# Sum of all eight probability tiles on VectorE, ones products of 256 columns, and a rotation whose sum is made by an adding transfer from GpSimd's queue

## What is computed

```
q = (lat @ Wq)                      # lat, ctx: layer norms of x and of the context
k, v = split(ctx @ Wkv)
k = apply_rope(k, cos, sin)         # x1*cos - x2*sin, x2*cos + x1*sin, on the halves of each head
attn = softmax(clip(q @ k.T * 64**-0.5, -11, 11))
x = x + (attn @ v) @ Wo + bo
x = x + sum over 16 experts of sigmoid(x @ sel) * relu(x @ keys) @ values    # x normalized first
```

## Time and profile before

| | us |
|---|---|
| median of 3 runs (1050.04 to 1054.57) | 1051.62 |
| the profiled execution | 1056.22 |
| its span | 1054.4 |
| TensorE busy | 994.2 |
| VectorE busy | 820.1 |
| ScalarE busy | 514.7 |
| GpSimd busy | 263.4 |

### The profile page before, as it was taken

The page is one execution under the profiler, slowest core; times in us unless marked ns, Lnnn a source line. Parts: engine busy times, 40 slices in busy tenths (PEclk is TensorE's granted clock), DMA queues, the critical chain, the costliest instruction groups (busy, mean ns, idle before and its releaser), DMA issues. The chain is left out here.

```text
span 1054.4 us, 15279 instructions
## 1 busy us (share of the span) xinstructions
PE 994.2 (94%) x5336; PEld 611.8 (58%) x5336; DVE 820.1 (78%) x1235; ACT 514.7 (49%) x759; POOL 263.4 (25%) x245
## 2 busy tenths in 40 slices
PE   4599999999999999999999999999998888999998
PEld 3455555555555555555555555555553366888886
DVE  5499988999999999999889988998899754545422
ACT  5465555555556556555555555555554422222221
POOL 5443423111112121111211000321000164445443
PEclk9899999999999999999999999999999889999999
DMA  6344323332323322223322234232223163332321
GB/s 171 117 138 126 104 82 106 96 91 66 91 78 112 93 72 86 72 89 87 97 67 81 61 89 114 91 90 82 61 62 101 46 209 137 121 121 83 122 95 40
DMA packets 69369, 101.39 MB, mean 96 GB/s; under 512 B 22000, under 2 KB 44784, under 8 KB 67248
## 3 DMA queue, kind: packets, MB, share of 16 engines
q1 hardware_dynamic: 69296, 100.46, 31.4%
HBM read 70.54 MB, written 10.75 MB: 77 GB/s over the span
## 5 line engine op out<-in xcount | busy, mean ns | idle before, releaser
L1016 ACT ACTIVATE probs<-score_ps 128x1024 f32<-128x1024 f32 x256 | 249.2, 1029 | 147.9 <-PE score_ps L829 147.8
L842 PE MATMUL o_ps<-probs,v_sb 128*64 128x512 f32 x1024 | 247.7, 605 | 0.0
L1222 DVE TENSOR_SCALAR probs<-probs 128x1024 f32<-128x1024 f32 x256 | 181.4, 739 | 75.8 <-ACT probs L1016 75.8
L1231 DVE TENSOR_TENSOR p_sum<-probs 128x1024 f32<-128x1024 f32 x128 | 161.7, 1264 | 2.3
L842 PEld LDWEIGHTS o_ps<-probs,v_sb 128*64 128x64 f32 x1024 | 62.2, 136 | 112.1 <-issue 93.3
L1777 DVE SCALAR_TENSOR_TENSOR act<-h_ps,sel_all 128x512 f32<-128x512 f32 x62 | 42.8, 690 | 101.1 <-PE h_ps L142 90.3
L829 PE MATMUL score_ps<-q_hi,k_hi 64*128 64x512 f32 x512 | 115.2, 446 | 1.1 <-DVE k_lo L1201 0.8
L829 PEld LDWEIGHTS score_ps<-q_hi,k_hi 64*128 64x128 f32 x512 | 48.2, 184 | 111.4 <-issue 98.0
L1693 ACT CAST act_hi<-act 128x512 fp32r<-128x512 f32 x64 | 39.6, 620 | 143.2 <-DVE act L1777 143.2
L1545 POOL TENSOR_TENSOR act_lo<-act,act_hi 128x512 fp32r<-128x512 f32 x64 | 82.5, 1290 | 102.8 <-ACT act_hi L1693 102.8
L829 PE MATMUL score_ps<-q_hi,k_lo 64*128 64x512 f32 x512 | 101.7, 393 | 0.0
(11 more groups left out here) (197 smaller groups left out, 1950.0 us busy)
## 6 DMA issues: line engine op xcount, KB each, us to landing
sel_all<-sel_dram SPq DMA_DIRECT2D x16, 1024.0 KB, 4.8
k_swap<-k SPq DMA_DIRECT2D x124, 128.0 KB, 2.3
w_hi<-packs_hi SPq DMA_DIRECT2D x26, 384.0 KB, 4.0
w_lo<-packs_lo SPq DMA_DIRECT2D x26, 384.0 KB, 4.5
den<-inv_dram SPq DMA_DIRECT2D x64, 128.0 KB, 2.9
ctx_raw<-ctx SPq DMA_DIRECT2D x24, 128.0 KB, 2.3
packs_hi<-w_hi SPq DMA_DIRECT2D x8, 384.0 KB, 3.3
packs_lo<-w_lo SPq DMA_DIRECT2D x8, 384.0 KB, 3.6
```

The source lines that it names most:

```text
L842: mm = pe.matmul(o_ps[DH * h:DH * h + DH, :], v_sb[n // 2 % 2][:, at:at + DH], probs[s % RING][:, h, :], start=(s == 0), stop=(s == STEPS ...
L1016: act.activation(probs[s % RING][:], score_ps[s % 2][:], ACT.Exp, scale=DH ** -0.5).then_inc(exp_done, 1)
L1222: dve.tensor_scalar(probs[s % RING][:], probs[s % RING][:], CLIP_HI, CLIP_LO, ALU.min, ALU.max).then_inc(clipped, 1)
L1231: dve.tensor_tensor(p_sum[m][:], first, second, ALU.add).then_inc(summed_up, 1)
```

## The change

Three things are changed together.

- VectorE adds the two quarter sums as well (`sum_all`, 128x1024, behind the second `sum_quad`), so that `p_sum[3]` holds all eight tiles. The four ones products now take 256 columns each: block e of a head the e-th half of the queries. `den`, `den_rows`, the turning and the copy of the denominators are halved accordingly, and `invert_den` has nothing to add.
- The sum of the rotation leaves VectorE. GpSimd's queue waits for both products (`k_times`) and starts a transfer that adds k_swap to k32 (`accum_op=ALU.add`, 512 KB). The rounding of k on ScalarE and the reuse of k_swap wait for that transfer (`k_summed`).
- The wait of `sum_up` for the ones products (`den_ready`) now stands at m = 3 alone.

```diff
--- before.py
+++ after.py
@@ -97,7 +97,7 @@
 
     sh.o_raw = sb("o_raw", [P, NQ])
     sh.den = sb("den", [P, NQ])
-    sh.den_rows = sb("den_rows", [P, 2, NQ // DH])
+    sh.den_rows = sb("den_rows", [P, NQ // DH])
     sh.inv_rows = sb("inv_rows", [P, NQ // DH])
     sh.o_hi1 = sb("o_hi1", [P, NQ], F32R)
     sh.o_lo1 = sb("o_lo1", [P, NQ], F32R)
@@ -114,7 +114,6 @@
     sh.den_evac = sem("den_evac")
     sh.ident_ready = sem("ident_ready")
     sh.den_turned = sem("den_turned")
-    sh.den_added = sem("den_added")
     sh.den_inv = sem("den_inv")
     sh.inv_stored = sem("inv_stored")
     sh.inv_spread = sem("inv_spread")
@@ -159,17 +158,15 @@
     for h in range(2):
         for e in range(2):
             at = DH * h + QUAD * e
-            row = sh.den[at:at + 1, :].rearrange("a (p j) -> a p j", p=DH)
-            sp.dma_start(sh.den_rows[DH * h:DH * h + DH, e, :], row).then_inc(sh.den_turned, DMA)
+            row = sh.den[at:at + 1, 0:NQ // 2].rearrange("a (p j) -> a p j", p=QUAD)
+            sp.dma_start(sh.den_rows[at:at + QUAD, :], row).then_inc(sh.den_turned, DMA)
 
 
 def invert_den(dve, sh, n):
 
     wait(dve, sh.den_turned, 4 * DMA * (n + 1))
     wait(dve, sh.inv_stored, DMA * n)
-    dve.tensor_tensor(sh.inv_rows[:], sh.den_rows[:, 0, :], sh.den_rows[:, 1, :], ALU.add).then_inc(sh.den_added, 1)
-    wait(dve, sh.den_added, n + 1)
-    dve.reciprocal(sh.inv_rows[:], sh.inv_rows[:]).then_inc(sh.den_inv, 1)
+    dve.reciprocal(sh.inv_rows[:], sh.den_rows[:]).then_inc(sh.den_inv, 1)
 
 
 def store_inv(sp, sh, inv_dram, n):
@@ -358,6 +355,7 @@
         half_times = [sem(f"half_times{i}") for i in range(2)]
         k_times = sem("k_times")
         k_roped = sem("k_roped")
+        k_summed = sem("k_summed")
         k_hi_done = sem("k_hi_done")
         k_split = sem("k_split")
         q_projected = sem("q_projected")
@@ -370,6 +368,7 @@
         clipped = sem("clipped")
         summed_up = sem("summed_up")
         quads_up = sem("quads_up")
+        all_up = sem("all_up")
         pv_done = sem("pv_done")
         head_loaded = sem("head_loaded")
         sel_zero = sem("sel_zero")
@@ -504,7 +503,8 @@
             def swap_k(p):
 
                 sp.wait_ge(k_evac, 2 * p + 2)
-                sp.wait_ge(k_roped, p + 1)
+                sp.wait_ge(k_roped, 2)
+                wait(sp, k_summed, DMA * (p - 1))
                 for q in range(4):
                     a, b = 32 * q, 32 * (q ^ 1)
                     sp.dma_start(k_swap[a:a + 32, :], k32[b:b + 32, :]).then_inc(k_swapped, DMA)
@@ -585,7 +585,7 @@
                 if n == 29:
                     store_gates(sp, sh, sel_dram, 0)
                 if n == NPAIR - 2:
-                    sp.wait_ge(k_roped, NPAIR + 1)
+                    sp.wait_ge(k_summed, DMA * (NPAIR - 1))
                     load_keys(2)
                     load_keys(3)
 
@@ -668,6 +668,11 @@
                 pool.wait_ge(half_swapped[half], 4 * DMA)
                 part = k_half(k_swap, half)
                 pool.tensor_tensor(part, part, k_half(sin_sb, half), ALU.mult).then_inc(half_times[half], 1)
+
+            def rope_add(p):
+
+                pool.wait_ge(k_times, 2 * p)
+                pool.dma_start(k32[:], k_swap[:], accum_op=ALU.add).then_inc(k_summed, DMA)
 
             def head_norm(t):
 
@@ -708,6 +713,8 @@
                 t, p = n + FIRST_TILES, n + 1
                 if t < TILES:
                     rstd(t)
+                if p < NPAIR:
+                    rope_add(p)
                 if n + 2 < PAIRS:
                     split_weights(n + 2)
                 if n % 2 == 0 and n // 2 + 2 < DUOS:
@@ -845,15 +852,15 @@
 
             def denominators(n):
 
-                pe.wait_ge(quads_up, 2 * n + 2)
+                pe.wait_ge(all_up, n + 1)
                 pe.wait_ge(ones_ready, 1)
                 wait(pe, den_evac, n)
                 wait(pe, y_added, 2 * (n - 1))
                 for e in range(2):
                     for h in range(2):
                         at = DH * h + QUAD * e
-                        mm = pe.matmul(side_ps[at:at + QUAD, :], ones[:], p_sum[2 * e + 1][:, h, :],
-                                       start=True, stop=True)
+                        mm = pe.matmul(side_ps[at:at + QUAD, 0:NQ // 2], ones[:],
+                                       p_sum[3][:, h, e * (NQ // 2):(e + 1) * (NQ // 2)], start=True, stop=True)
                 mm.then_inc(den_ready, 1)
 
             def turn_first(t):
@@ -1002,7 +1009,7 @@
                 act.copy(v_sb[j % 2][:, at:at + 512], fill_bank(f)[:]).then_inc(v_stored, 1)
 
             def round_k(p):
-                act.wait_ge(k_roped, p + 2)
+                act.wait_ge(k_summed, DMA * p)
 
                 wait(act, scores_ready, STEPS * (p - 1))
                 act.copy(k_hi[p % 2][:], k32[:]).then_inc(k_hi_done, 1)
@@ -1024,7 +1031,7 @@
                 act.wait_ge(den_ready, n + 1)
 
                 wait(act, o_scaled, n)
-                act.copy(den[:], side_ps[:]).then_inc(den_evac, 1)
+                act.copy(den[:, 0:NQ // 2], side_ps[:, 0:NQ // 2]).then_inc(den_evac, 1)
 
             def round_weights(w):
 
@@ -1191,10 +1198,6 @@
                 dve.tensor_tensor(k32[:], k32[:], cos_sb[:], ALU.mult).then_inc(k_times, 1)
                 dve.tensor_tensor(k_swap[:], k_swap[:], sin_sb[:], ALU.mult).then_inc(k_times, 1)
 
-            def rope_add(p):
-                dve.wait_ge(k_times, 2 * p)
-                dve.tensor_tensor(k32[:], k32[:], k_swap[:], ALU.add).then_inc(k_roped, 1)
-
             def split_k(p):
 
                 dve.wait_ge(k_hi_done, p + 2)
@@ -1225,7 +1228,7 @@
             def sum_up(n, m):
 
                 dve.wait_ge(clipped, STEPS * n + 2 * m + 2)
-                if m % 2 == 1:
+                if m == 3:
                     wait(dve, den_ready, n)
                 first, second = (probs[(2 * m + j) % RING][:] for j in range(2))
                 dve.tensor_tensor(p_sum[m][:], first, second, ALU.add).then_inc(summed_up, 1)
@@ -1235,6 +1238,11 @@
                 dve.wait_ge(summed_up, MACROS * n + 2 * half + 2)
                 first, second = p_sum[2 * half], p_sum[2 * half + 1]
                 dve.tensor_tensor(second[:], first[:], second[:], ALU.add).then_inc(quads_up, 1)
+
+            def sum_all(n):
+
+                dve.wait_ge(quads_up, 2 * n + 2)
+                dve.tensor_tensor(p_sum[3][:], p_sum[1][:], p_sum[3][:], ALU.add).then_inc(all_up, 1)
 
             dve.wait_ge(power_ready, 3)
             stats(0)
@@ -1306,8 +1314,6 @@
             def iteration(n):
                 p, t = n + 1, n + FIRST_TILES
                 for m in range(MACROS):
-                    if m == 2 and p < NPAIR:
-                        rope_add(p)
                     if m == 3 and n >= 2:
                         add_y(dve, sh, n - 2, 1, side_ps, bo)
                     clip(n, 2 * m)
@@ -1316,6 +1322,7 @@
                         split_q(p)
                     if m == 0 and n > 0:
                         sum_quad(n - 1, 1)
+                        sum_all(n - 1)
                     sum_up(n, m)
                     if m == 0:
                         if t < TILES:
@@ -1353,6 +1360,7 @@
             for n in range(NPAIR):
                 iteration(n)
             sum_quad(NPAIR - 1, 1)
+            sum_all(NPAIR - 1)
             split_o(dve, sh, NPAIR - 2, 0)
             split_keys(3)
             for mt in range(2):
```

## The result

The changed kernel takes 1236.37 us (median of 4 runs, 1233.81 to 1241.03) against 1052.09 (median of 4, 1050.04 to 1054.57): a ratio of 1.1762, 95% interval 1.1739 to 1.1785, or 184 us more. The profiled execution took 1233.81 us with a span of 1232.0 and a granted TensorE clock of 0.927.

The account below looks back on a forecast made before the run. VectorE's chain with its ScalarE detour was taken as the bound. 31 x (T - 1.60) + 7 - 4 gave +146 us at T = 6.2, on the 1051.62 median 1197 us; range 1098 to 1280, the forecast's own 1130 to 1235.

Parts of the forecast that it names:

- T: Time from the end of the second rotation product until k32 holds the sum; assumed 6.2 us.
- rival 3: VectorE's clips of tiles 4 and 5 hold up GpSimd's transfer descriptors: T 7.5, +40 us more, 1237 us; chance 0.20.
- The bound: Head-pair loop: VectorE's in-order chain with its detour over ScalarE sets the 24.45 us period; TensorE, 94% busy, waits.
- 31T - 46.6: Total added time: 31 iterations of T - 1.60 us, plus 7, minus 4; +146 us at T = 6.2.
- the prediction's own extra term: While tiles are normalized, clips 6 and 7 wait on ScalarE's work behind k_hi: 0.4 us average, 17 times, 7 us.
- The copy of the denominators: ScalarE detour: copying 256 columns instead of 512 saves between 0 and half of a 0.59 us copy; taken as 0.
- GpSimd's splits behind the wait: First six iterations: weight splits queue behind the products' wait, delaying later loads; costed at nothing, 8 us if T is small.
- VectorE's additions: VectorE gains sum_all and loses rope_add, 1.14 us each: sum 0; the small denominator addition, 0.20 us, goes.
- 1 (quick transfer): The adding transfer takes T from 1.9 to 4: 1098 us at T = 3.0, 1064 at 1.9; chance 0.14.
- 5 (T near 1.6): Nothing to measure, as the transfer's delay per iteration cancels at T near 1.6; chance 0.03.
- 2 (a gain): Sum lands within T = 1.40 us: 0.20 us less per iteration, 1045 us, or 1038 if TensorE bounds; chance 0.03.
- 4: TensorE's clock falls to half speed after about 3 us standing still: 1.5 us more per iteration, 1243 us; chance 0.08.

Follow-up runs that it names:

- e1: Kernel before with only the denominators' part (VectorE sums all eight tiles, ones products of 256 columns); rotation's sum stays on VectorE: 1072.28 us, ratio 1.0198.
- e9: Kernel before with ScalarE's copies of output and denominators moved behind exponentials 2 and 3, invert_den behind the rotation's products: 1047.47 us, ratio 0.9967.
- e5: e4 with GpSimd issuing the adding transfer only after VectorE has clipped tiles 4 and 5: 1198.83 us, ratio 1.1415.
- e3: Changed kernel with each packed-weight fetch cut to its first 16 columns, so later pairs use wrong weights: 1163.01 us, ratio 1.1076.
- e4: Changed kernel with SyncE issuing the packed-weight fetches only after the rotation's sum has landed, nothing left out: 1157.26 us, ratio 1.1020.
- e7: e4 with a plain copy from ScalarE's queue in place of GpSimd's adding transfer, leaving out the first rotation product: 1119.82 us, ratio 1.0650.
- e6: e4 with a plain copy from GpSimd's queue in place of the adding transfer, leaving out the first rotation product: 1122.02 us, ratio 1.0681.
- e2: Changed kernel with the denominators' part undone (512-column ones products, small addition back), adding transfer kept: 1219.29 us, ratio 1.1597.
- e8: Changed kernel with a GpSimd addition instruction (128x1024) in place of the adding transfer: 1126.90 us, ratio 1.0724.

## Why the prediction was right

Forecast 1197, measured 1236: inside the range of 1098 to 1280, but 1 us above the forecast's own 1130 to 1235, and in the band (T above 7.4) that the prediction gave to rival 3. The direction and the path of the delay are as foretold; the time that came of it was a quarter more, 184 us for 146. By its steps:

- *The bound.* Right. VectorE's chain with the detour sets the period (e1), and TensorE waits; with the detour moved, TensorE takes over (e9). In the last nine iterations that is less clear (e1).
- *T.* This is the term that was mis-sized: 6.2 assumed, 7.65 on average. The nearest rows were copies out of the loop; one number was put on two situations. Alone the adding transfer gives T = 5.0, which is 0.3 to the issue, 3.4 of a plain copy and 1.3 for the adding; beside the fetches it is 6.3 to 9.8. "It starts when the next weight packs are being fetched" stood in the prediction, and had no price of its own: 72 to 78 us. T = 6.2 lies between the two situations and is that of neither.
- *The sum, 31T - 46.6.* Right in what matters, the 31 T; the rest closes in part because its errors cancel. With each run's own T, and 0.21 x 31 = 6.5 us taken off for the copy (known from e1, so after the event), it gives:

| run | mean T | by the formula | measured loss |
|---|---|---|---|
| after | 7.65 | 184 | 185 |
| e5 | 6.54 | 150 | 149 |
| e3 | 5.38 | 114 | 113 |
| e4 | 5.26 | 110 | 107 |
| e7 | 3.83 | 66 | 68 |
| e6 | 3.78 | 64 | 72 |

  By stretches, what a period has grown by beyond T - 1.60 is 0.33 to 0.39 us from iteration 5 to 20 in after and e3 to e7, with a mean T from 3.7 to 8.1 there; the prediction's own extra term was 0.4. From iteration 21 on it is -0.7 to -1.0, some 8 us in all, where the prediction took off 4. In the first five it is -0.3 to +0.2, but 0.8 in e7 and 1.2 in e6.

  For e2, which has neither sum_all nor the shorter copy and keeps the small addition, it is 31 x (T - 2.54) + 3 = 167, measured 168.
- *The copy of the denominators, taken as 0.* It was 0.21 us an iteration (bounds 0 and 0.3).
- *GpSimd's splits behind the wait.* Taken as nothing while T is long, 8 us if it is short. `scale_o` waited for the inverse denominators 3.0 us in all in the changed kernel up to 209 us, and 6.7 in e6, where T is short: right in kind and about right in size. e6's first five periods average 28.4 us, against 29.2 in e4, though T is 1.9 us shorter there; from the sixth on the 1.3 us come back in full. It is not all of that shortfall, since e7 has no such wait and shows 0.8 us an iteration too.
- *VectorE's additions.* sum_all against rope_add, 0 together: VectorE's busy time is nearly unchanged, 822.3 against 820.1. The denominators' part alone (e1) costs 21 us.
- *What was to be seen.* k_lo's pause "near 4.8 us": 177.9 / 31 = 5.7. k_hi's "about 5": 238.3 / 31 = 7.7. The landing "about 6": 7.5. The period "near 29": 31.34. Ones products at about 0.5 us with a wait: 0.57 (512.61 to 513.18, where the scores begin) and 1.03.
- *The rivals.* 1 (quick transfer) and 5 (T near 1.6) fell on size: T is never under 4.9. 2 (a gain) fell in e1 and after. 3 named 1237, and the time is there, but its cause gives 0.1 to 0.4 us an iteration and not 1.3 (e5, e6): a time alone does not tell which rival was right. 4: the fact came, clock 0.50 behind a wait of 6.33 us, and the wait was twice the 3 us foretold, but the price did not come: what a period has beyond T - 1.60 is the same 0.33 to 0.39 us whether TensorE waits long (after) or short (e7), and clips 0 and 1 wait for nothing.

Open: why GpSimd's transfer moves its first packets only 2.2 to 4.7 us after the issue in most iterations with fetches under way, against 1.5 to 2.0 alone; and what bounds the last nine iterations, which absorb most of what e1 adds.

## What to carry to other kernels

A transfer put on an engine's critical chain costs its whole latency, however few instructions it saves: here 1.1 us of VectorE were bought with a delay of 5.0 us, and of 7.65 in company. Price such a transfer with what else the DMA queues carry in that very stretch, and order the deferrable ones (weights for later) behind it by a wait; that alone was worth 78 us of 184. And a busy share of 94% does not name the bound: VectorE, at 78%, set the period here; look for the chain in which every pause is its own work coming back.

## What the runs showed of the hardware

- A transfer of 512 KB from on-chip memory to on-chip memory lands in 3.4 us from GpSimd's queue (e6) and 3.5 from ScalarE's (e7; medians); adding, in 4.7 (e4); adding beside fetches of 768 KB and more, in 7.5, at most 9.5 (after). The fetches suffer as well: 5.6 and 6.4 us for 384 KB instead of 3.3 and 4.1.
- VectorE's clips beside GpSimd's issue hold it until 0.1 us after a clip's end: an issue of 1.03 us instead of 0.53, a landing of 3.4 instead of 3.0 to 3.1 (e6). A gap of 0.07 us between two clips let it through.
- An addition of 128x1024 on GpSimd, 2.4 us, keeps VectorE's clips out until it ends: 3.43 us for two clips instead of 1.29 (e8).
